# Offsets clamped by VectorE between two bounds per row, without ScalarE's distance pass

## The reference

```python
def _block(x, dc_w, dc_b, of_w, of_b, dw, db):
    h = jax.nn.relu(_deconv2d(x, dc_w, dc_b))
    offset = _conv2d(h, of_w, of_b, PAD)
    return jax.nn.relu(_deform_conv2d(h, offset, dw, db))
```

```python
py = base_y.astype(x.dtype) + off[:, :, 0]
px = base_x.astype(x.dtype) + off[:, :, 1]
sampled = jax.vmap(_bilinear_sample)(x, py, px)
wk = w.reshape(w.shape[0], w.shape[1], -1)
return jnp.einsum('bckhw,ock->bohw', sampled, wk) + b[None, :, None, None]
```

## Time and profile before

| | us |
|---|---|
| median of 3 runs | 4314.02 |
| lowest, highest run | 4310.0, 4314.37 |
| profiled execution, its span | 4314.1 |

### The profile page before, as it was taken

The page is one execution under the profiler, slowest core; times in us unless marked ns, Lnnn a source line. Parts: engine busy times, 40 slices in busy tenths (PEclk is TensorE's granted clock), DMA queues, the critical chain, the costliest instruction groups (busy, mean ns, idle before and its releaser), DMA issues.

```text
span 4314.1 us, 221726 instructions
## 1 busy us (share of the span) xinstructions
PE 3880.1 (90%) x81908; PEld 2973.5 (69%) x81908; DVE 2952.5 (68%) x5858; ACT 2786.4 (65%) x6651; POOL 1140.5 (26%) x645
## 2 busy tenths in 40 slices
PE   4998799699789879979988997998799999799998
PEld 3776577477567657756765775776577777577776
DVE  5885687488567668847856884784577774577775
ACT  2885588388478658837865883885355554255554
POOL 0441243134033214403322431331111110111111
PEclk8999899799989989989998997999799999899999
DMA  4442544344244334424424443443766664666664
GB/s 125 127 127 66 143 125 110 89 126 127 75 132 126 90 106 127 125 76 131 126 71 127 127 114 92 126 125 109 179 154 152 150 150 127 147 154 152 152 150 110
DMA packets 244838, 533.50 MB, mean 124 GB/s; under 512 B 61200, under 2 KB 151824, under 8 KB 227216
## 3 DMA queue, kind: packets, MB, share of 16 engines
q1 hardware_dynamic: 194224, 498.67, 45.0%
q10 hardware_dynamic: 50240, 29.89, 2.4%
HBM read 471.87 MB, written 56.45 MB: 122 GB/s over the span
## 4 chain that ended last, share of the span: by engine, by line
PE 68%; SPq 18%; issue 7%; ACT 2%; DMA 2%; DVE 2%; POOLq 0%; ACTq 0%; DVEq 0%; POOL 0%; PEld 0%; PEldq 0%
PE P L544 26%; PE PS L562 24%; SPq L380 9%; PE P L515 8%; PE PS L575 8%; SPq L388 8%; SPq L370 1%; PE PS L515 1%; ACT H L848 1%; DMA X<-x_dram 1%; PE P L530 1%; DVE FOFF L1032 1%; DMA VT<-ht_store 0%; DVE A L917 0%; DVE ST L1036 0%
## 5 line engine op out<-in xcount | busy, mean ns | idle before, releaser
L917 DVE TENSOR_TENSOR A<-P,YC 121x384 f32<-121x384 f32 (+1 forms) x4608 | 2311.4, 550 | 850.1 <-ACT YC L768 684.5
L544 PE MATMUL P<-HL,SEL 32*121 32x384 f16 (+1 forms) x21504 | 1745.6, 304 | 131.6 <-issue 95.3
L768 ACT ACTIVATE YC<-P 121x384 f32<-121x384 f32 (+1 forms) x4608 | 1733.9, 444 | 98.7 <-PE P L544 65.8
L544 PEld LDWEIGHTS P<-HL,SEL 32*121 32x121 f16 (+1 forms) x21504 | 1126.9, 117 | 513.9 <-issue 228.6
L562 PE MATMUL PS<-A,VT 121*32 121x80 f32 (+1 forms) x40960 | 1342.7, 250 | 51.7 <-DMA VT<-ht_store 15.5
L562 PEld LDWEIGHTS PS<-A,VT 121*32 121x32 f32 (+1 forms) x40960 | 1093.0, 117 | 354.6 <-issue 200.4
L1103 POOL CAST HL<-DIST 128x1152 f16<-128x1152 f32 x320 | 366.3, 1145 | 3066.1 <-DVE DIST L922 3043.8
L745 ACT ACTIVATE SMP<-PS 128x480 f32<-128x480 f32 (+3 forms) x1152 | 593.9, 516 | 638.2 <-PE PS L562 632.9
L1105 POOL TENSOR_TENSOR HL<-DIST,HL 128x1152 f16<-128x1152 f32 x320 | 769.6, 2405 | 58.5 <-POOL HL L1103 58.5
L735 ACT ACTIVATE DIST<-HB,CONST 128x1152 f32<-128x1152 f32 x320 | 400.8, 1252 | 231.4 <-DMA HB<-off_store 128.8
L575 PE MATMUL PS<-SMP,CW 128*64 128x128 f32 x7424 | 476.0, 277 | 5.4 <-ACT SMP L745 5.4
(11 more groups left out here) (61 smaller groups left out, 703.4 us busy)
## 6 DMA issues: line engine op xcount, KB each, us to landing
HB<-off_store SPq DMA_DIRECT2D x2560, 72.0 KB
VT<-ht_store SPq DMA_DIRECT2D x256, 512.0 KB
VT<-ht_store SPq DMA_DIRECT2D x768, 132.0 KB
VT<-ht_store SPq DMA_DIRECT2D x256, 88.0 KB
off_store<-FOFF SPq DMA_DIRECT2D x160, 128.0 KB, 2.6
H<-x_dram SPq DMA_DIRECT2D x5, 2048.0 KB, 14.6
ht_store<-A ACTq DMA_DIRECT2D x32, 256.0 KB, 3.3
ht_store<-VT ACTq DMA_DIRECT2D x32, 256.0 KB, 3.9
```

Of the source, the lines that this page charges most:

```text
L544: mm = nc.tensor.matmul(dst, SEL[q, table, 0:sh.npos], hats, start=part == 0, stop=part == 1)
L768: nc.scalar.activation(YC[0:sh.npos, g % X_SLOTS, 0:sh.size], P[0:sh.npos, g % Y_SLOTS, 0:sh.size], ACT.Copy).then_inc(y_ready, 1)
L917: return nc.vector.tensor_tensor(dst, x, y, ALU.mult)
```

## The change

The hat max(0, 1 - |d|) is now made as a difference of two ramps. For each row of HB (a window position q) DVE clamps the offset between SCALE * (q - MARGIN - 1) and SCALE * (q - MARGIN), two columns of CONST read as row scalars (`STEP_FROM`, `STEP_TO`); a table that holds 1 for a position and -1 for the next one turns two such ramps into a hat. So:

- ACT's distance pass (L735) goes, with its semaphore `abs_done`. The clamp reads HB directly, waits for the load of HB and for POOL to have done with the DIST of the chunk before (`hats_full`), and SP's offset loads wait for `clamp_done`.
- SEL has neighbouring differences: two more DVE operations in each step's prefix, and other tables from the host. The fallback has tables of its own.
- A spread now gives the hat less SCALE. For x the product adds it, (P + SCALE) * YC, as a SCALAR_TENSOR_TENSOR; for y the eviction does, with a scale of 1/SCALE^2 and a bias of 1/SCALE (column `ONE` of CONST), as an Identity activation.
- The residual stands behind the seventh product (g = 6) in shape 0, and as before in shape 1.
- The lower end of the range is at most -2 instead of -1. SEL grows from 640 to 1024 columns, CONST from 14 to 17.

```diff
+        self.add_after = self.sum_after + (5 if kind == 0 else 2)
...
-        HAT_BIAS = CONST[:, LAYERS + 1:LAYERS + 2]
+        STEP_FROM = CONST[:, LAYERS + 10:LAYERS + 11]
+        STEP_TO = CONST[:, LAYERS + 11:LAYERS + 12]
+        ONE = CONST[:, LAYERS + 12:LAYERS + 13]
...
                 def next_offsets(c, band, half):
 
-                    sp.wait_ge(abs_done, c - 1)
+                    sp.wait_ge(clamp_done, c - 1)
                     load_offsets(band, half)
...
-            def distance(band, half):
-
-                wait_alone(act, hb_full[half], 32 * IMG * (band + 1))
-                nc.scalar.activation(DIST[:, :], HB[:, half, :], ACT.Abs, bias=HAT_BIAS).then_inc(abs_done, 1)
-
...
-                            if sh.kind == 0 and g == sh.next_at and not last:
-                                next_distance(c + 1, band + half, 1 - half)
                             act.wait_ge(y_full, n + 1)
 
                             act.wait_ge(product_done, n + 1)
                             nc.scalar.activation(YC[0:sh.npos, g % X_SLOTS, 0:sh.size], P[0:sh.npos, g % Y_SLOTS, 0:sh.size],
-                                                 ACT.Copy).then_inc(y_ready, 1)
-                            if sh.kind > 0 and b == 0 and g == sh.next_at and not last:
-                                next_distance(c + 1, band + half, 1 - half)
+                                                 ACT.Identity, bias=ONE[0:sh.npos], scale=1.0 / SCALE ** 2).then_inc(y_ready, 1)
...
-                return nc.vector.tensor_tensor(dst, x, y, ALU.mult)
-
-            def clamp(c):
-
-                dve.wait_ge(abs_done, c + 1)
-                nc.vector.tensor_scalar(DIST[:, :], DIST[:, :], SCALE, SCALE, ALU.min, ALU.subtract).then_inc(clamp_done, 1)
+                if sh.kind == 2:
+                    return nc.vector.tensor_tensor(dst, x, y, ALU.mult)
+                return nc.vector.scalar_tensor_tensor(dst, x, SCALE, y, ALU.add, ALU.mult)
+
+            def clamp(c, band, half):
+
+                if not isinstance(c, int):
+                    dve.wait_ge(hats_full, c)
+                wait_alone(dve, hb_full[half], 32 * IMG * (band + 1))
+                nc.vector.tensor_scalar(DIST[:, :], HB[:, half, :], STEP_FROM, STEP_TO, ALU.max, ALU.min).then_inc(clamp_done, 1)
...
-                                clamp(c + 1)
-                            if before >= sh.lag and b == sh.batches - 1 and g == sh.sum_after + 2:
+                                clamp(c + 1, band + half, 1 - half)
+                            if before >= sh.lag and b == sh.batches - 1 and g == sh.add_after:
...
-                    counted(nc.vector.tensor_scalar(SEL[:, axis, :], REL[:, axis, :], ST[:, 34 + axis:35 + axis], 1.0 / SCALE,
-                                                    ALU.is_equal, ALU.mult))
+                    counted(nc.vector.tensor_scalar(TMP[:, axis, :], REL[:, axis, :], 1.0, ST[:, 34 + axis:35 + axis],
+                                                    ALU.subtract, ALU.is_equal))
                 chained()
+                for axis in range(2):
+                    counted(nc.vector.scalar_tensor_tensor(SEL[:, axis, :], REL[:, axis, :], ST[:, 34 + axis:35 + axis], TMP[:, axis, :],
+                                                           ALU.is_equal, ALU.subtract))
```

More of the change, by code:

```diff
@@ L142, in build @@
         REL = sb("REL", [128, 2, 128])
-        SEL = sb("SEL", [128, 5, 128], F16)
+        SEL = sb("SEL", [128, 8, 128], F16)
         BIAS = sb("BIAS", [128, 3 * (LAYERS + 1)])
-        CONST = sb("CONST", [128, LAYERS + 1 + 1 + 4 + 4])
+        CONST = sb("CONST", [128, LAYERS + 1 + 1 + 4 + 4 + 3])
         FAR = sb("FAR", [128, CPX + CHUNKS + 16])
@@ L185, in build @@
         hb_full = [sem(f"hb_full{i}") for i in range(2)]
-        abs_done = sem("abs_done")
         clamp_done = sem("clamp_done")
@@ L199, in build @@
         stepwise = [conv_full, conv_act, conv_dve, ht_full, ht_copied, ht_stored, off_full, off_ready, *off_stored, range_done,
-                    flag_step, *hb_full, abs_done, clamp_done, hat_step, hats_full, y_full, y_ready, x_full, product_done,
+                    flag_step, *hb_full, clamp_done, hat_step, hats_full, y_full, y_ready, x_full, product_done,
                     *vt_full, ps_full, ps_free, res_done, turn]
@@ L466, in step @@
                 load_offsets(0, 1)
-                sp.wait_ge(abs_done, 1)
+                sp.wait_ge(clamp_done, 1)
                 load_offsets(1, 0)
@@ L655, in fallback @@
                             pe.wait_ge(turn, base + T["spread", g])
-                            spread(sh, g, 0, 0, 4, 0)
-                            spread(sh, g, 0, 0, 2, 1)
-                            spread(sh, g, 0, 0, 3, 2).then_inc(turn, 1)
+                            spread(sh, g, 0, 0, 7, 0)
+                            spread(sh, g, 0, 0, 5, 1)
+                            spread(sh, g, 0, 0, 6, 2).then_inc(turn, 1)
                         for k in range(BLOCKS):
@@ L752, in read_sum @@
                     out_act(layer, PS[:, :], half, final).then_inc(ps_free, 1)
-                def next_distance(c, band, half):
-                    wait_alone(act, hats_full, c)
-                    distance(band, half)
                 def body(c, band, half, before, last):
@@ L855, in step @@
                             store_ht(unit, n)
-                distance(0, 0)
                 sampling(act, bar_count, final, lambda sh: body_of(sh, layer, final),
@@ L1058, in step @@
                 flag_count[0] += 1
-                clamp(0)
+                clamp(0, 0, 0)
                 chained()
@@ L1075, in step @@
                 chained()
-                counted(nc.vector.tensor_scalar(ST[:, 34:36], ST[:, 32:34], -1.0, None, ALU.min))
+                counted(nc.vector.tensor_scalar(ST[:, 34:36], ST[:, 32:34], -2.0, None, ALU.min))
                 chained()
@@ L1128, in _tables @@
     rel = np.full((128, 2, 128), 99.0, np.float32)
-    sel = np.zeros((128, 5, 128), np.float32)
+    sel = np.zeros((128, 8, 128), np.float32)
     for axis in range(2):
@@ L1137, in _tables @@
         for n in range(16 * columns):
-            sel[:, 2 + tile, first + n] = is_x & (q == j + LANES * (n % columns))
-            sel[:, 4, first + n] = ~is_x & (q == n // columns)
+            for of, table, mine in ((j + LANES * (n % columns), tile, is_x), (n // columns, 2, ~is_x)):
+                after = 1.0 * (mine & (q == of + 1)) if of + 1 < AXIS else 1.0 * (MARGIN - AXIS + 1) / MARGIN * (mine & (q == 0))
+                sel[:, 2 + table, first + n] = 1.0 * (mine & (q == of)) - after
+                sel[:, 5 + table, first + n] = (mine & (q == of)) / SCALE
     pxc = np.zeros((STRIPES, CH, STRIPE_ROWS, COLS), np.float32)
@@ L1143, in _tables @@
         pxc[:, AXIS + k] = (np.arange(COLS) % BLK)[None, :] + k % 3 - 1
-    consts = np.zeros((128, LAYERS + 1 + 1 + 4 + 4), np.float32)
+    consts = np.zeros((128, LAYERS + 1 + 1 + 4 + 4 + 3), np.float32)
     consts[:, 0:5] = [0.0, 1.0, 1.0, 0.0, 1.0]
-    consts[:, 5] = SCALE * (MARGIN - q)
     consts[:, 6:10] = -1e30
@@ L1150, in _tables @@
     consts[:, 10:14] = [BOUND1, BOUND1 - 3.0, BOUND1, BOUND1 - 3.0]
+    consts[:, 14], consts[:, 15], consts[:, 16] = SCALE * (q - MARGIN - 1), SCALE * (q - MARGIN), 1.0 / SCALE
     far = np.zeros((128, CPX + CHUNKS + 16), np.float32)
@@ L1155, in _tables @@
     far[:, CPX + CHUNKS:] = -np.where(is_x[:, None], 16 * (window % 4) + q[:, None], 16 * (window // 4) + q[:, None])
-    return dict(sel=(sel / SCALE).astype(np.float16).reshape(128, -1), rel=rel.reshape(128, -1),
+    return dict(sel=sel.astype(np.float16).reshape(128, -1), rel=rel.reshape(128, -1),
                 pxc=(SCALE * pxc).reshape(128, -1), consts=consts, far=SCALE * far)
```

## The result

Changed kernel: 4333.59 us, median of 5 runs (4325.06 to 4351.48); before: 4314.02 (4306.95 to 4314.37, 5 runs). The ratio is 1.0051, 95% interval [1.0038, 1.0064]: slower by half a per cent. That is inside the stated range, 4298 to 4340, and 4.6 us above the forecast's own, 4309 to 4329. The profiled execution took 4325.06 us, its span is 4323.3 (a run's time is 1.8 us longer than its span).

A forecast was written before the change was run, and what follows sets the result against it. It took SyncE's queue (8.55 us a chunk) to bound the mid steps, with consumers slightly slower, and TensorE the final layer. 4314.1 - 12.4 (mid steps) + 16.3 (final layer) = 4318.0 us; own range 4309 to 4329, stated range 4298 to 4340.

The forecast's parts named there:

- Mid steps: The eight steps of layers 0 to 3: 13.95 us of lag won, mostly step 0, less 1.6 for late evictions: -12.4 us.
- the lag: Mid steps, chunk 29: time from the end of window issues to first sample matmul; 6.21 us in step 0, floor 2.22.
- Rival B: Mid chunks: ACT's 1.14 us of longer evictions lie on the consumers' path; slower, 4332 to 4366 us; chance 0.16.
- Evictions, +95 ns: ACT: the bias pointer adds 95 ns to each of 12 evictions in a mid chunk, 1.14 us.
- Clamp: DVE: row scalars instead of immediates make it 830 ns instead of 751; bounds 0.68 to 0.91 us.
- rival D: DVE: the clamp loses its rate, 1.36 us for 1152 elements; slower, 4350 us; chance 0.09 together with rival C.
- rival C: DVE: the product in its new form is slowed beside POOL, +0.28 us; 4414 us; chance 0.09 together with rival D.
- The residual's price: DVE: moved three products later, the residual still takes 0.62 us beside POOL and 0.34 without; worth 0.
- (a): Final layer, from chunk to chunk: one longer eviction on the path, 2 x 31 x 0.093 = 5.8 us slower.
- (b): Final layer, at the clamp: longer eviction and clamp delay products, 0.175 us each time, 2 x 30 x 0.175 = 10.5 us.
- Rival A: Final layer takes up the longer evictions and clamp, 0 to 4 of the 16 us; faster, 4303 us; chance 0.30.
- the price of the clock: Mid steps: TensorE clock drops after waits for windows; put at 0, upper bound 8 x 1.7 = 14 us.

The follow-up runs named there:

- the second: Second trace: the changed kernel once more, unaltered, run for another trace; 4334.08 us, ratio 1.0053 to the kernel before.

## Why the prediction was right, and where it was off

- Mid steps: forecast -12.4, measured -14.0 and -11.4, by the mechanism named: the lag fell to 2.2 us, then SyncE's queue bounds, and the gain is all in the first groups. Two paces on the way there were misread. The present one was taken as 8.69, from a lag grown over 29 chunks, and is 8.59; the lag of step 0 was there from the start (5.81 us at chunk 2). The one to come was taken as 8.0, from a last chunk that has no clamp either, and is 8.39, still under 8.55, so the error cost nothing. Rival B, which decides from 8.55, missed by 0.16 us a chunk.
- Evictions, +95 ns: 94 and 89. Clamp: 870 ns where 830 was taken, within its bounds, so rival D did not come. Product: unchanged at 551, so rival C did not come. The Trainium skill ("SBUF — State Buffer", section "Who interferes with whom") says that a VectorE instruction with at most one SBUF input, outside the two-port modes, does not contend with GpSimd. The trace agrees: the product of shape 0, with one input in PSUM, takes 556 ns beside POOL's subtraction and 549 clear of POOL. The residual's price did not stay, as the prediction had it (733 ns for 559); that cost no time.
- Final layer (a): one eviction's 0.093 us a chunk, measured 0.09. (b): 0.175, measured 0.21; the clamp's part, taken as 0.08, is 0.13 (0.88 with immediates against 0.75 before). Together 31 x 2 x 0.09 + 30 x 2 x 0.21 = 18.2 us against 16.3. Rival A fell: the final layer does not take them up.
- What failed is the price of the clock, "so I put it at 0, upper bound one such drop at the end of each step". It was looked for in the mid steps, where TensorE waits for windows 109 times, and the first trace has one drop there. It lies in the final layer, at the places (a): 5 drops of 1.2 us in the first trace, 9 in the second, 2 to 11 in the other kernels whose evictions read a column, all behind meetings of the longer kind, and none in the traces of before and of the four other kernels whose evictions read none (the one with merged loads, which waits for transfers throughout, left aside). With it the sum of the first trace is 4314.1 - 14.0 + 18.2 + 6.0 = 4324.3 (span 4323.3). The timed runs are 2 to 28 us above that span. Drops may be part of this spread: the mean granted clock is 0.940 in the fastest run and 0.935 in the slowest. It isn't shown, and they are not all of it, since the kernel with immediates, with no such drop in its trace, spreads from 4302.5 to 4322.0.
- The measured time is in the range, but above 4309 to 4329, which the forecast's own sum allowed. The range reached up to 4340 to take in the near end of rival B, which did not come; that it took in the drops too is luck.
- The Trainium skill ("TensorE: Matmul & The Clock Gate", section "A second HAM failure mode: psum-queue depth-cycling") has frequent short idles between groups of matmuls make the clock swing. The traces do not bear it out as it stands: the meeting shown idles 0.29 us and is followed by a drop, the same meeting before idles 0.36 and is not, and the waits of mid chunks are followed by one drop in the first trace. The drop of the earlier trace rows, which the prediction took as agreeing, came behind one wait of 0.91 us for a transfer, not behind frequent short idles. What in the longer meeting makes the clock fall stays open; that the column in the evictions brings it is shown by taking the column out and by putting it in.

## What to carry to other kernels

A pass taken off an engine is worth what the next bound leaves over: here 11 to 14 of 50 us, since a transfer queue ran just beside the old pace. A small price put on each of many instructions is read at the places where a chain goes through them, not from the engine's busy sum: ACT's sum fell, and a chunk of the final layer got longer by the price of two evictions and of the clamp. Here Identity with a constant column costs 0.09 us more an eviction than Copy with an immediate, and the clamp could be put into idle time a product earlier.

## What the runs showed of the hardware

- With evictions that read a column, the longer meetings of the final layer went from 2.67 to 2.74 us, and TensorE's clock fell to 1.2 GHz behind 2 to 11 of 26 of them in six traces, at 1.2 to 1.5 us each; in five traces without the column (the one with merged loads left aside) it fell behind none, though TensorE idled no less there (0.36 us before, 0.29 with the column).
- Four transfers of 32 rows from a three-level source kept SyncE's queue busy for 7.6 to 8.3 us, with one or two packets under way at a time; eight of 16 rows with the same bytes took 3.84 us, with up to sixteen.
- The residual, with both inputs in SBUF, took 342 ns clear of POOL, 612 beside its cast and 957 on average beside its subtraction; the product, with one input in PSUM, 549 and 556.
